# Attention kernel: inverse softmax sums spread over partitions by DMA through outside memory instead of by selector products on TensorE

## The reference

```
c_kv = h @ w_down_kv.T
q = rope(c_q @ w_up_q.T);  k = rope(c_kv @ w_up_k.T);  v = c_kv @ w_up_v.T
scores = einsum('bhqd,bhkd->bhqk', q, k) / sqrt(64)
attn = softmax(scores, axis=-1)                 # exp(scores - max) / sum
out = einsum('bhqk,bhkd->bhqd', attn, v)        # 16 heads
out = out.reshape(b, s, 1024) @ w_out.T + residual
```

## Time and profile before

| | |
|---|---|
| median of 3 runs | 1083.81 us (1083.73 to 1083.85) |
| the profiled execution's own time | 1083.63 us |
| its span, first to last instruction | 1081.8 us |
| mean granted TensorE clock | 0.993 of full |
| busy share of the span | PE 96%, ACT 86%, DVE 83%, POOL 83% |
| DMA | 217.96 MB, 201 GB/s on average |

### The profile page before, as it was taken

How to read it: one execution, slowest core, us unless ns; L and a number is a source line. 1 busy time by engine, 2 the same in 40 slices (tenths; PEclk the granted TensorE clock), 3 DMA queues, 4 the chain that set the end, 5 groups by cost and what they waited for, 6 DMA issues and landing times.

```text
span 1081.8 us, 26191 instructions
## 1 busy us (share of the span) xinstructions
PE 1041.4 (96%) x6880; PEld 700.7 (65%) x6880; DVE 898.9 (83%) x1223; ACT 930.0 (86%) x3136; POOL 895.9 (83%) x897
## 2 busy tenths in 40 slices
PE   3789999999999999999999999999999999999987
PEld 2556666666666666666666666666666666666654
DVE  3798888898888889888889888889888888888872
ACT  3789988988998888999898999898899889898861
POOL 3777989888888888888898888988888988888851
PEclk9899999999999999999999999999999999999999
DMA  5388777877877877777887777787777787777773
GB/s 178 106 227 207 204 209 202 223 211 200 205 208 204 230 203 207 206 202 202 219 215 207 203 203 209 201 228 208 199 208 206 203 229 204 210 195 196 207 193 81
DMA packets 93281, 217.96 MB, mean 201 GB/s; under 512 B 22464, under 2 KB 43200, under 8 KB 93120
## 3 DMA queue, kind: packets, MB, share of 16 engines
q1 hardware_dynamic: 92864, 216.52, 75.5%
q10 hardware_dynamic: 384, 1.05, 0.4%
HBM read 7.77 MB, written 4.19 MB: 11 GB/s over the span
## 4 chain that ended last, share of the span: by engine, by line
PE 80%; issue 6%; DVE 6%; SPq 3%; ACT 2%; DMA 2%; ACTq 0%; DVEq 0%; POOL 0%; POOLq 0%
PE ps_s L328 20%; PE ps_u L342 20%; PE ps_b L447 10%; PE ps_qk L318 8%; PE ps_a L383 5%; PE ps_a L396 5%; PE ps_qk L319 4%; SPq L254 3%; PE ps_b L413 2%; DVE turned L703 2%; DVE qk L687 2%; PE ps_a L355 1%; PE ps_a L360 1%; PE ps_b L456 1%; PE ps_a L367 1%
## 5 line engine op out<-in xcount | busy, mean ns | idle before, releaser
L538 ACT ACTIVATE prob<-ps_s,neg_max 128x256 f32<-128x256 f32 x1024 | 475.0, 486 | 41.0 <-DVE neg_max L692 38.2
L837 POOL TENSOR_TENSOR partner<-partner,rope_sb 128x512 f32<-128x512 f32 x256 | 327.1, 1278 | 108.3 <-DMA partner<-raw 108.3
L692 DVE TENSOR_REDUCE neg_max<-ps_s 128x4 f32<-128x1024 f32 x256 | 310.8, 1214 | 116.9 <-PE ps_s L328 115.4
L840 POOL TENSOR_TENSOR qk<-qk,partner 128x512 f32<-128x512 f32 x256 | 326.5, 1275 | 20.1
L703 DVE STREAM_TRANSPOSE turned<-prob 128x1024 f32<-128x1024 f32 x256 | 316.4, 1236 | 2.3 <-ACT prob L538 1.3
L328 PE MATMUL ps_s<-qk 64*128 64x256 f32 x2048 | 292.4, 404 | 3.5 <-ACT prob L538 2.4
L342 PE MATMUL ps_u<-gathered,ckv 128*64 128x256 f32 x2048 | 278.4, 393 | 3.1 <-DMA gathered<-turned 2.8
L328 PEld LDWEIGHTS ps_s<-qk 64*128 64x128 f32 x2048 | 177.5, 187 | 106.0 <-issue 86.5
L538 ACT ACTIVATION_READ_ACCUMULATOR prob<-ps_s,neg_max 128x1 f32 x1024 | 221.8, 217 | 0.0
L550 ACT COPY raw<-ps_qk 128x512 f32<-128x512 f32 x256 | 154.1, 602 | 67.0 <-PE ps_qk L319 66.9
L342 PEld LDWEIGHTS ps_u<-gathered,ckv 128*64 128x64 f32 x2048 | 124.8, 136 | 107.8 <-issue 52.6
(11 more groups left out here) (67 smaller groups left out, 897.5 us busy)
## 6 DMA issues: line engine op xcount, KB each, us to landing
gathered<-turned SPq DMA_DIRECT2D x1016, 128.0 KB, 2.4
partner<-raw SPq DMA_DIRECT2D x256, 256.0 KB, 2.4
x_sb<-in_x SPq DMA_DIRECT2D x32, 128.0 KB, 2.3
resid<-early SPq DMA_DIRECT2D x32, 128.0 KB, 2.0
out<-out_sb SPq DMA_DIRECT2D x32, 128.0 KB, 2.1
turned<-in_wup SPq DMA_DIRECT2D x2, 512.0 KB, 5.7
gathered<-turned ACTq DMA_DIRECT2D x8, 128.0 KB, 4.0
rope_sb<-in_rope SPq DMA_DIRECT2D x1, 512.0 KB, 6.8
```

Source lines behind the costliest of these rows:

```text
L538: last = nc.scalar.activation(prob[:, s % 2, :, h, :, t, :].rearrange("p j k c -> p k j c"), ps_s[:, s % 2, h, t, :].rearrange("p (k j c) ...
L692: nc.vector.tensor_reduce(neg_max[:, s % 2, :, :], ps_s[:, s % 2, :, :, :], AXIS_X, ALU.max, negate=True).then_inc(max_ready, 1)
L837: nc.gpsimd.tensor_tensor(other, other, sin_sb, ALU.mult).then_inc(sin_ready, 1)
L840: nc.gpsimd.tensor_tensor(qk[:, s % 4, :, :], qk[:, s % 4, :, :], other, ALU.add).then_inc(rope_done, 1)
```

## The change

The selector products, the transposes of the inverse sums on PE, their copies on ACT and the splitting on POOL go. DVE inverts the sums at step 0 of the batch (before: step 4) and turns them by one 32 by 32 block transpose, after which a partition holds 32 tokens of one head. SP writes that tile (16 KB) to a tensor `rows_out` in the chip's outside memory at step 1, ahead of the 12 moves of that step, and at step 3 reads it back with two DMAs of 512 KB, each of which repeats 8 KB over 64 partitions. The result, `spread`, now holds all four quarters. POOL multiplies a batch's quarters at step 7 and at steps 0, 1 and 2 of the next, PE's output products stand in steps 1, 3, 4 and 6, behind the other products of the step. `den` is laid out by head halves so that the two DMAs are contiguous. The 512 KB selector matrix is neither loaded nor cast.

```diff
+            def keep_rows(b, par, i):
+                sp.wait_ge(rows_ready, done(b))
+                if not outside(b - 2, B):
+                    sp.sem_inc(sp_waited, 1)
+                    sp.wait_ge(spread_in[par], 32 * i)
+                sp.dma_start(rows_out[par].rearrange("h (t q c) -> q (h t) c", t=TT, c=32),
+                             rden_t[:, :]).then_inc(rows_kept[par], 16)
+
+            def spread_rows(b, par, i):
+                sp.wait_ge(rows_kept[par], 16 * (i + 1))
+                sp.sem_inc(sp_waited, 1)
+                sp.wait_ge(u_norm, done(CHUNKS * (b - 1) + CHUNKS - 1))
+                for h in range(2):
+                    sp.dma_start(spread[h * L:(h + 1) * L, :, :].rearrange("p j s -> p (j s)"),
+                                 rows_out[par, h * PAIRS:(h + 1) * PAIRS, :].rearrange("j s -> (j s)").unsqueeze(0)
+                                 .to_broadcast([L, PAIRS * S])).then_inc(spread_in[par], 16)
...
+                if not outside(b, B):
+                    if p == 1:
+                        keep_rows(b, b0, i)
+                    elif p == 3:
+                        spread_rows(b, b0, i)
...
-            def transpose_rden(b):
...
-            def broadcast_rden(b, c):
...
-                    pe.wait_ge(bc_evac, done(CHUNKS * b + CHUNKS - 1))
+                    pe.wait_ge(final_done, done(b - 1))
                 pe.wait_ge(u_norm, done(CHUNKS * b + c))
...
-                if not outside(b - 1, LAST) and p >= 4:
-                    attention_out(b - 1, p - 4, 1 - b0)
...
-                if p < 4 and not outside(b - 1, LAST):
-                    broadcast_rden(b - 1, p)
                 if not outside(b, B) and p in (2, 3):
                     ffn_out(b, p - 2)
+                if not outside(b - 1, LAST) and p in (1, 3, 4, 6):
+                    attention_out(b - 1, (1, 3, 4, 6).index(p), 1 - b0)
...
-            def copy_spread(b, c):
...
-            def copy_rden(b):
...
-                nc.scalar.copy(sel_sb[:, :, :], sel_raw).then_inc(setup_act, 1)
...
+            def invert_sums(b, b0, i):
                 dve.wait_ge(exp_done, done(PAIRS * b + PAIRS - 1))
-                dve.wait_ge(rden_split, done(b - 1))
-                nc.vector.reciprocal(rden[:, :, :], den[:, b0, :, :]).then_inc(rden_ready, 1)
+                nc.vector.reciprocal(rden[:, :], den[:, b0, :, :].rearrange("p h t -> p (h t)")).then_inc(rden_ready, 1)
+                dve.wait_ge(rden_ready, done(b))
+                if not outside(b - 1, B):
+                    dve.sem_inc(dve_waited, 1)
+                    dve.wait_ge(rows_kept[1 - b0], 16 * (i + b0))
+                    dve.sem_inc(dve_waited, 1)
+                nc.vector.transpose(rden_t[:, :], rden[:, :]).then_inc(rows_ready, 1)
...
-            def split_sums(b):
...
-            def normalise_u(b, c, par):
-                pool.wait_ge(bc_evac, done(CHUNKS * b + c))
+            def normalise_u(b, c, par, n):
+                pool.wait_ge(spread_in[par], 32 * (n + 1))
...
-                if p in (1, 2, 4, 5) and not outside(b - 1, LAST):
-                    normalise_u(b - 1, {1: 0, 2: 1, 4: 2, 5: 3}[p], 1 - b0)
+                if p < 3 and not outside(b - 1, LAST):
+                    normalise_u(b - 1, p + 1, 1 - b0, i - 1 + b0)
+                if p == 7 and not outside(b, LAST):
+                    normalise_u(b, 0, b0, i)
```

More of the change, by code:

```diff
@@ L521, in step @@
                     transpose_sum(b - 1)
-                if p == 7 and not outside(b, LAST):
-                    transpose_rden(b)
             run(pe, prologue, step)
@@ L657, in step @@
                     copy_u(g, s, i)
-                if p == 0 and not outside(b - 1, LAST):
-                    copy_spread(b - 1, 0)
                 if p == 0:
@@ L764, in finish @@
                 dve.wait_ge(fin_ready, done(b))
-                if not outside(b + 1, B):
-                    dve.wait_ge(rt_ready, done(b + 1))
                 dve.wait_ge(copied[par], 16 * (i + 1))
@@ L813, in step @@
                             integrate(b, b0, k)
-                        if not is_last(b):
-                            invert_sums(b, b0)
+                if p == 0 and not outside(b, B):
+                    invert_sums(b, b0, i)
                 if is_last(b):
-                    if p == 0:
-                        invert_sums(b, b0)
-                    elif p == 5:
-                        normalise_last(b, 0, b0)
-                        normalise_last(b, 1, b0)
-                    elif p == 6:
-                        normalise_last(b, 2, b0)
+                    if p == 6:
+                        for c in range(2):
+                            normalise_last(b, c, b0, i)
+                    elif p == 7:
+                        normalise_last(b, 2, b0, i)
                 elif is_last(b - 1):
@@ L880, in normalise_u @@
                 two = u_sb[:, par, 2 * c:2 * c + 2, :]
-                nc.gpsimd.tensor_tensor(two, two, spread[:, c % 2, :, :], ALU.mult).then_inc(u_norm, 1)
+                nc.gpsimd.tensor_tensor(two, two, spread[:, 2 * c:2 * c + 2, :], ALU.mult).then_inc(u_norm, 1)
             def prologue():
@@ L893, in step @@
                 b = i * UNROLL + b0
-                if p == (1 if is_last(b) else 5) and not outside(b, B):
-                    split_sums(b)
                 if not outside(g + LEAD["rope"], STEPS):
@@ L920, in rope_tables @@
     return np.ascontiguousarray(np.stack([one * scale, one], 2))
-def head_selectors():
-    sel = np.zeros((P, PAIRS, P), np.float32)
-    for pair in range(PAIRS):
-        for h in range(2):
-            for part in range(2):
-                sel[part * H + 2 * pair + h, pair, h * L:(h + 1) * L] = 1.0
-    return sel
 def kernel(**inputs):
```

121 lines of the change are left out of this document (29 added, 92 removed).

## The result

The changed kernel takes 1146.52 us (median of 4, 1144.88 to 1149.30), the kernel before on the same chip 1083.77: the ratio is 1.0582, 95% interval 1.0561 to 1.0603. It was forecast at 1057 with a range of 1034 to 1084, so the time is 62 us beyond the slow end of the range, on the other side of "no change". Of the rivals only B forecast a slower kernel.

A forecast was written before the change was run, and what follows sets the result against it. PE was taken to bound the kernel at 32.1 us a batch; 1.6 off gives 30.5, late moves add 0.9 for 31.4. Over 30 batches that saves 21 us, plus 6 at the end: 1083.63 to 1057 us, range 1034 to 1084.

The forecast's parts named there:

- Rival B: Reads of one 8 KB row into 64 partitions take longer: at 8 us, period 33.1 and 1108 us; chance 0.14.
- What bounds it before: Steady batches: PE never stands still, and its products one behind the other take 32.1 us a batch.
- Off PE, 1.6 us a batch: Selector products (1.3 us) and transposes (0.32) leave PE, so PE alone needs 30.5 us a batch, 48 us over batches 1 to 30.
- SP's issue: Three more DMAs in SP's queue: from step 0's moves to step 5's twelve takes 27.3 us, which just fits.
- DMA time of the reads, 4.6 us: The two reads behind step 3's exchange take the DMA engines 4.6 us, so the last move lands 1.85 us late.
- The delay of 1.85 counts once in two batches: At step 0 PE's product is late, but that step's moves are not; every second batch catches up, making the period 31.4 us.
- POOL: Step 7's exchange starts 0.7 us into the next batch; POOL's rotation for step 6 is done at 22.5, barely fitting.
- Rival C: The small write holds step 1's twelve moves in every batch: 0.5 us gives period 30.6, 2.1 gives 32.2; chance 0.12.
- Last batch, -6 us: At the end, ACT's waits (about 3 us), eight selector products (about 1) and PE's tail (some 2) go: 6 us, between 2 and 9.
- A: The reads hide, at 400 GB/s or with faster catching up: period 30.6 to 30.8, 1036 us; chance 0.26.
- D: SP's issues of the reads cost far more than 0.6 us: at 1.5 each, period again about 31.4, same as the forecast.
- anything else: Any outcome outside the forecast and its lettered rivals, counted as faster; chance 0.02.

The follow-up runs named there:

- e9: The changed kernel with neither the write nor the reads from the third batch on (output wrong): 1053.99 us, ratio 0.9712.
- e12: As e6, with the write moved from step 1 to step 3 and output products at steps 3, 4, 6 and 7: 1102.58 us, ratio 1.0175.
- e4: The changed kernel with the reads taking 64 different rows of 8 KB instead of one row 64 times (output wrong): 1147.41 us, ratio 1.0540.
- e11: The changed kernel with the write going out as 128 rows of 128 bytes, slowest dimension 128 instead of 4 (output wrong): 1145.14 us, ratio 1.0574.
- e13: The kernel before plus only two reads of 512 KB a batch into an unused tile, at step 7: 1110.80 us, ratio 1.0233.
- e14: The changed kernel with the write behind step 1's moves, each read halved between steps 3 and 7, POOL's multiplications at steps 7, 0, 2, 4: 1090.00 us.
- e16: As e14, but each half is one transfer to 128 partitions, all from the first head group (output wrong): 1080.36 us, ratio 0.9938.
- e2: The changed kernel with each read bringing half the bytes from the third batch on (output wrong): 1073.56 us, ratio 0.9917.
- e7: The changed kernel with ACT instead of SP issuing the reads, at the end of its step 3: 1259.88 us, ratio 1.1605.
- e8: The changed kernel with ACT issuing the reads at the end of its step 7: 1134.26 us, ratio 1.0478.
- e6: The changed kernel with SP issuing the reads behind step 7's exchange, output products and multiplications later: 1108.85 us, ratio 1.0217.

## Why the prediction was wrong, step by step

- **What bounds it before: right.** PE never waited in the steady part, and without the new transfers it is again busy for 399.15 us of 400 (e9, 300 to 700).
- **Off PE, 1.6 us a batch: too much.** e9 measured 32.08 - 30.96 = 1.1. The traces show about half of the missing 0.5. In e9 the weights of the first product L407 wait for DVE's count in about half the batches (3.7 us in 16 times); periods of 31.06 and 30.87 us alternate, which is 0.1 on average. And the output products did not quite "cost as much as before", which is 0.16: from the start of a quarter to PE's next start it is now 0.95 us three times and 0.86 once, before it was 0.96 once and 0.87 three times. The rest was not found.
- **SP's issue: right.** From the exchange of step 1 to the end of the last move it takes 25.06 us; the sum had 27.3 less the four moves and a gap, 24.7. A read costs 0.57, the write 0.61 in place of 0.45.
- **DMA time of the reads, 4.6 us: mis-sized.** 5.5 us (e12 against before and e9). The profiles' pages agree for the whole run: SP's queue took 86.7% of 1144.9 us, before 75.5% of 1081.8, which is 5.5 us in each of 32 batches.
- **"The delay of 1.85 counts once in two batches": this is the step that failed.** I followed the moves of step 0, whose `turn` is early, and concluded that they do not shift. But ahead of the twelve moves in SP's queue stands the exchange of step 1, which needs `raw` of step 1, and PE makes that behind the late product. The queue is in order, so the whole delay returns in every batch. With the forecast's own sizes that would have been 30.5 + 1.85 = 32.35 us and 1085 us in all, just beyond its range; 0.9 more for the reads makes 33.25, and 33.5 was measured. An estimate of the whole gap of 89 us between forecast and time: some 72 are the periods (33.96 on average against 31.4, 28 of them), 18 the end.
- **POOL: a landing left out.** I followed the exchange of step 7 and not that of step 5, which stands directly behind the reads. POOL waited 3.83 us for it and PE 1.02; in the chain of the middle batches it costs nothing beside the moves, and what it cost in the first six was not separated.
- **Rival B: right sign, wrong cause.** Its circle was the same halved one, and its cause (many partitions reading one address) is refuted by e4.
- **Rival C: partly.** The write does stand in the circle in every batch, as C said; not by occupying the queue (e11), but by SP's time, and only beside the reads.
- **Rivals A and D: no.** The reads did not run at 400 GB/s (5.5 us of all engines in place of 2.6), and a read's issue cost SP 0.57 us, not 1.5.
- **Last batch, -6 us: wrong sign, +11.6.** Two waits of 6.18 and 3.17 us for `gathered` came in, and the granted clock was 0.80. Without the new transfers the gain is there: the end of e9 takes 88.4 us, 4.2 less than before. The wait of 3.20 us that the forecast counted on was ACT's own time for issuing four moves:

```profile
1056.68 3.39 ACTq L624 DMA_DIRECT2D gathered<-turned  x4
```

- **Slips in its sums, of no weight.** By its own numbers no gain is left from a period of 32.3 us on, not 32.4 (rivals B and C), and its 0.78 for faster leaves out the 0.02 of anything else that it counts as faster. The sums of SP's issue, of the DMA work and of POOL come out as stated.

What stays open: the circle is read from the traces, and no run takes the exchange of step 1 alone out of it. Open is also why PE waits longer in the first six batches than later, in the changed kernel and in e13, what keeps e12 and e14 at 32.2 us, and why a read to 64 partitions needs 5.5 us where its bytes at the 400 GB/s of the earlier trace rows need 2.6; the number of partitions explains 1.4 of it (e16).

## What to carry to other kernels

When a transfer is late, follow every instruction that the waiting engine issues next, until one of them gates the same queue again. If one does, the delay is paid in each turn of the loop and not averaged. And trading 1.1 us of the fullest engine for 5.5 us of one that is at 0.79 is only free if the sum stays clearly below the period and no waited-for transfer stands behind the burst.

## What the hardware showed

- A waited-for transfer pays for the backlog in its queue: a move landed after 2.4 us in e2 and after 5.4 at the chain's end in the changed kernel. The queue of another engine was no way out: four moves took SP 4.18 us to issue in place of 2.5 (e7), and with the reads at step 7 it cost 25 us more than SP's own queue (e8 against e6).
- The slowest dimension of a source can decide: reads of 2 x 64 x 4 KB took the kernel to 1697.71 us, 128 x 4 KB to 1080.36; but for a write of 16 KB, 4 against 128 made no difference (e11).
- The granted clock can fall right after PE has waited, and then makes the wait cost again: 0.50 from 96 to 98 us in e9 after 2.8 us of standing still. A wait of that length need not do it: in the changed kernel PE stood still for 2.81 us ahead of 93.63, and the clock was 1.00 in the same two us (first row); but it was 0.50 from 636 to 638, behind a wait of 2.24 (second row). In the middle of the changed kernel, with waits of 1.0 and 1.4 us in a batch, it was 1.00 in the window shown.

```profile
96.00:98.00 2.00, 2.00 (x16) 1.34 (x15) 2.00 (x2) 1.56 (x6) 1.92 (x2) 1.00 0.04 14
...
636.00:638.00 2.00, 2.00 (x10) 1.82 (x8) 2.00 (x3) 1.22 (x4) 1.92 (x3) 0.50 0.97 266
```
